# Padding rows of a routed expert layer: sixteen small stores of one engine's queue, divided between two queues

## The reference, cut to what matters

```
x = x + 0.5 * ffn(layernorm(x))
x = x + attention(layernorm(x))      # ALiBi, causal, 16 heads
x = x + 0.5 * ffn(layernorm(x))

def ffn(x):                          # E = 16 experts, each token goes to TOP_K = 4
    t = rmsnorm(x) * norm_w
    vals, idx = top_k(t @ gate_w.T + gate_b, 4)
    gates = softmax(vals)
    h = t @ w1[e] + b1[e]            # 2 * 256 columns, interleaved a and b
    act = min(a, 7) * sigmoid(1.702 * min(a, 7)) * (clip(b, -7, 7) + 1)
    return x + sum over the 4 chosen e of gates * (act @ w2[e] + b2[e])
```

## Time and profile before

| | us |
|---|---|
| median of 3 runs | 1021.15 |
| lowest, highest | 1018.97, 1021.18 |
| the profiled execution | 1019.23 |
| its span, first to last instruction | 1017.5 |
| TensorE matmuls busy | 722.9 (71%) |
| VectorE busy | 610.9 (60%) |
| ScalarE busy | 445.6 (44%) |
| GpSimd busy | 328.3 (32%) |

### The profile page before, as it was taken

The page is one execution under the profiler, slowest core; times in us unless marked ns, Lnnn a source line. Parts: engine busy times, 40 slices in busy tenths (PEclk is TensorE's granted clock), DMA queues, the critical chain, the costliest instruction groups (busy, mean ns, idle before and its releaser), DMA issues.

```text
span 1017.5 us, 22304 instructions
## 1 busy us (share of the span) xinstructions
PE 722.9 (71%) x5722; PEld 428.6 (42%) x5722; DVE 610.9 (60%) x1961; ACT 445.6 (44%) x974; POOL 328.3 (32%) x356
## 2 busy tenths in 40 slices
PE   2222079999899917778889488487129999999930
PEld 2111046666565613223343243244116666666620
DVE  6778235666555564787787368347305666665647
ACT  2534035555555524357465235261015555555510
POOL 3667713333333314101111600605512333333320
PEclk9999999999999966889999788797559999999975
DMA  9754345555444253631201313315333333333148
GB/s 311 261 212 161 136 118 167 168 168 169 131 136 127 76 176 93 197 116 49 80 18 53 132 45 130 131 44 202 118 106 99 98 99 101 95 96 91 50 133 280
DMA packets 120111, 131.63 MB, mean 129 GB/s; under 512 B 39596, under 2 KB 101525, under 8 KB 119864
## 3 DMA queue, kind: packets, MB, share of 16 engines
q1 hardware_dynamic: 101656, 91.11, 29.9%
q0 software_dynamic: 13728, 34.64, 9.5%
q10 hardware_dynamic: 4608, 4.46, 1.2%
HBM read 69.54 MB, written 64.21 MB: 131 GB/s over the span
## 4 chain that ended last, share of the span: by engine, by line
PE 44%; SPq 14%; DVE 13%; issue 13%; ACT 5%; another core or an unknown queue 5%; ACTq 3%; DMA 3%; DVEq 0%; POOLq 0%; POOL 0%
PE banks L407 13%; PE banks L429 6%; SPq L218 3%; ACT w2s L1434 3%; SPq L232 3%; SPq L217 2%; PE banks L1211 2%; PE banks L1165 2%; DVE X L727 2%; SPq L230 2%; PE banks L1277 2%; PE banks L1235 2%; PE banks L403 2%; PE banks L416 2%
## 5 line engine op out<-in xcount | busy, mean ns | idle before, releaser
L341 POOL DMA_INDIRECT y_rows<-y,goal x158 | 155.6, 985 | 318.5 <-ACT y L499 296.0
L407 PE MATMUL banks<-w1s,rT 128*128 x948 | 233.7, 383 | 0.0
L689 DVE TENSOR_SCALAR pbh<-banks 128x256 f32<-128x256 f32 x158 | 67.1, 425 | 197.3 <-ACT pbh L485 125.9
L1597 DVE CUSTOM_DVE_ANT_0 pbh<-banks,maskq 128x128 bf16<-128x128 f32 (+3 forms) x256 | 114.0, 487 | 77.8 <-PE banks L1188 46.3
L1434 ACT ACTIVATE w2s<-banks 128x1024 f32<-128x1024 f32 (+3 forms) x128 | 89.7, 701 | 123.4 <-PE banks L1219 84.3
L407 PEld LDWEIGHTS banks<-w1s,rT 128*128 128x128 f16 x948 | 93.7, 99 | 97.2 <-issue 4.0
L429 PE MATMUL banks<-w2s,hsT 128*128 x948 | 129.2, 273 | 0.0
L478 ACT ACTIVATE rT<-banks 128x512 f16<-128x512 f16 x158 | 93.5, 593 | 42.7 <-issue 34.7
L485 ACT ACTIVATE pbh<-banks 128x256 f32<-128x256 f32 x158 | 60.5, 383 | 117.3 <-PE banks L407 113.9
L1125 POOL DMA_INDIRECT x_rows<-row,row_to x64 | 61.7, 964 | 121.8 <-DVE row_to L1731 103.5
L389 PE MATMUL banks<-ident,row 128*128 128x128 f16 x632 | 62.6, 223 | 51.2 <-DMA goal<-x_rows 50.4
(11 more groups left out here) (238 smaller groups left out, 1059.7 us busy)
## 6 DMA issues: line engine op xcount, KB each, us to landing
row<-x_rows SPq DMA_DIRECT2D x158, 128.0 KB
arena<-in_w SPq DMA_DIRECT2D x16, 512.0 KB, 7.1
w1s<-y_rows SPq DMA_DIRECT2D x16, 512.0 KB, 4.7
arena<-y_rows SPq DMA_DIRECT2D x16, 512.0 KB, 7.8
qk_split<-w1s SPq DMA_DIRECT2D x48, 128.0 KB
arena<-qk_split SPq DMA_DIRECT2D x64, 96.0 KB, 2.3
w_lent<-w1s SPq DMA_DIRECT2D x22, 256.0 KB
w1s<-w_lent SPq DMA_DIRECT2D x11, 512.0 KB
```

Source lines behind the costliest of these rows:

```text
L341: pool.indirect_dma_start(y_rows[m], bass.IndirectOffsetOnAxis(ap=goal[:, n % NG, :], axis=0), y[:, n % NY, :], None, bounds_check=K * T - ...
L407: mm = pe.matmul(o, rT[:, n % 2, 2 * r + k, :], w1s[:, bass.ds(e, 1), k, w, :], start=False, stop=(k == HC - 1 and w == 1))
L689: dve.tensor_scalar(b[:, n % 2, :], bank[2 + n % 2][:, INNER:], (LIMIT + 1.0) * S, (1.0 - LIMIT) * S, ALU.min, ALU.max).then_inc(each("b"), 1)
L1597: dve.tensor_tensor_reduce(junk[:, (n * U + j) % 3, 0:W], query_bank[(n * U + j) % 3][:, 0:W], maskq[:, SEQ - W:], 1.0, -3e38, ALU.add, AL ...
```

## The change

The 16 paddings of each layer are divided. ScalarE issues those of experts 0 to 7, at the same place of its program in layer 0. In layer 1 it does so at the start of its part of the layer, that is behind the load of its gelu table and no longer ahead of it. SyncE issues those of experts 8 to 15, one behind the row loads of each of the first eight slots of a layer. The semaphores `padded` are the same in both layers, so that layer 1 waits for 64 more. The wait for all 16 in `rows_ready` is gone; instead the loads of the first 16 slots wait in groups of four in layer 1 too.

```
+PADS_FIRST = 8
+            padded = [sem(f"padded{c}") for c in range(4)]
-                padded = [ev(f"padded{c}") for c in range(4)]
+            def pad_rows(eng, e):
+                first = eng.value_load(pad_at[0:1, e:e + 1], min_val=0, max_val=(E - 1) * REGION + T)
+                eng.dma_start(x_rows[m][bass.ds(first, P), :], pad[:, :]).then_inc(padded[e // 4], 16)
...
-                    if m == 0 and n < E:
-                        sp.wait_ge(padded[n // 4], 64)
+                    if n - FIRST < E:
+                        sp.wait_ge(padded[(n - FIRST) // 4], m * 64 + 64)
...
                     load_rows(n, *(places[n] if n in places else place_of(n)))
+                    if n - FIRST < E - PADS_FIRST:
+                        pad_rows(sp, PADS_FIRST + n - FIRST)
...
                 act.preload_act_table_set("gelu_apprx_sigmoid_and_others")
-                if m == 0:
-                    act.wait_ge(route("pad_at"), 1)
-                    for e in range(E):
-                        first = act.value_load(pad_at[0:1, e:e + 1], min_val=0, max_val=(E - 1) * REGION + T)
-                        act.dma_start(x_rows[m][bass.ds(first, P), :], pad[:, :]).then_inc(padded[e // 4], 16)
+                act.wait_ge(route("pad_at"), m + 1)
+                for e in range(PADS_FIRST):
+                    pad_rows(act, e)
                 rows_out(FIRST)
...
-                sp.wait_ge(s("padded"), E * 16)
...
-                act.wait_ge(route("pad_at"), 2)
-                for e in range(E):
-                    first = act.value_load(pad_at[0:1, e:e + 1], min_val=0, max_val=(E - 1) * REGION + T)
-                    act.dma_start(x_rows[1][bass.ds(first, P), :], pad[:, :]).then_inc(s("padded"), 16)
```

## The result

The changed kernel takes 1028.57 us (median of 12 runs, 1020.05 to 1033.12) against 1021.16 (12 runs, 1016.27 to 1025.32): ratio 1.007, 95% interval 1.0042 to 1.0097. It is slower by 7.4 us. Its profiled execution took 1031.05 us with a span of 1029.3, which is 11.8 more than the span of before.

The account below looks back on a forecast made before the run. The prediction took SyncE's issue rate to bound layer 0, and in layer 1 ScalarE's paddings to delay the first row load. Layer 0 +8.6 and layer 1 -4.7 gave +3.9 us, 1025.0 against the median 1021.15, range 1016.5 to 1029.0.

Parts of the forecast that it names:

- What bounds the kernel: SyncE's issue rate sets the end of layer 0: 3.14 us a slot against TensorE's 2.72.
- Layer 0, ScalarE: Opening of layer 0: ScalarE free at 124.4, TensorE starts 4.1 us earlier, at 129.7; counts nothing in the sum.
- SyncE's start stays: Layer 0: SyncE's first row load stays at 124.07, as the paddings beside its place reads remain on ScalarE.
- The price of a padding: Each padding costs SyncE's queue 1.07 us, so eight cost it 8.6 us.
- The body of layer 0: Layer 0 to slot 69: slot time taken as unchanged, so every load behind the paddings comes 8.6 us later.
- the calm lock: Rival, 22%: SyncE and GpSimd issues don't collide in layer 0; layer 0 costs +2.5, net -2.2, 1019.0 us.
- the bad lock: Rival, 12%: slots of some 3.25 us over layer 0's lent slots; +13.4 and -4.0, about 1030.5 us.
- Layer 1: Layer 1's first load comes 8.05 us earlier, SyncE's paddings take most back; slot 8 turned 4.7 earlier, bounds 7.0 and 4.0.
- Groups of four: Waiting for paddings in groups of four on SyncE's queue costs nothing; a padding lands within 1.75 us.
- The sum: Layer 0 +8.6, layer 1 -4.7, together +3.9 us: 1025.0 against the median; own range 1022 to 1028.
- The rule of the skill: Initiating a DMA is usually small beside the DMA; by it the paddings would cost layer 0 nothing.
- the rival of free paddings: Rival, 12%: transfers, not issues, pace layer 0, which keeps its end; layer 1 gains 4.7 to 7.0, about 1015.5 us.

Follow-up runs that it names:

- e3: Kernel before, with two register reads added on SyncE behind each of the first eight row loads of layer 0, no padding moved: 975.03 us, ratio 1.0095.
- e5: Kernel before, with the two halves of each lent w1 stored by one DMA, 11 DMAs fewer on SyncE: 955.96 us against 965.09, ratio 0.9911.
- e11: Kernel before, with the 22 lent stores of layer 0 joined and issued by ScalarE instead of SyncE: 1021.65 us against 1029.40, ratio 0.9923.
- e8: Kernel before, with ScalarE's sixteen paddings of layer 0 held back until all scatters there have landed: 971.53 us, ratio 1.0063.
- e2: Kernel before, with the paddings divided in layer 0 alone, layer 1 as before: 975.35 us, ratio 1.0104.
- a2: The changed kernel run once more, same code, in the calm condition: 978.57 us against 965.09 for the kernel before, ratio 1.0143.
- e1: Kernel before, with the change in layer 1 alone, ScalarE issuing all 16 paddings in layer 0: 970.37 us against 964.85, ratio 1.0055.
- b2: Kernel before, no edit, profiled again in the slow condition: one execution, 1031.46 us.
- s1: Kernel before, with one more register read ahead of each of ScalarE's 16 paddings in layer 1: 1035.72 us against 1029.40, ratio 1.0061.
- e10: e5 with all 16 paddings on ScalarE, waited for in groups of four in both layers, layer 1's behind the gelu table load: 957.09 us, ratio 0.9915.

## Why the prediction was right, point by point

The direction came true, and for layer 0 the mechanism. The size did not: +7.4 us where +3.9 was forecast. The time lies 0.43 us inside the upper end of the range, and that it lies inside at all is partly luck.

*What bounds the kernel.* Right. That SyncE's queue sets the end of layer 0 is shown by e3 (reads alone, +8.8 us to slot 8 and +10 us in the time), e5 and e11 (instructions taken away, 9.1 and 7.8 us faster), and e8 (TensorE's start 13.5 us later, the time only 6.4).

*Layer 0, ScalarE.* Forecast 5.6 us from the first row load to the first up product, measured 5.25; worth nothing, as said.

*SyncE's start stays.* Nearly. It is 126.89, but everything began 3.9 us late; counted from the first padding it is 1.1 us earlier. That says nothing, since unsplit kernels in the same condition have 13.8 to 18.7 us between the two (16.9 in before). In the calm condition it is 20.0 to 20.1 us whether ScalarE has eight paddings (e2, a2) or sixteen (e1).

*The price of a padding* was the term most under-sized: 1.07 us forecast. In the changed kernel the distances of the row loads of slots 0 to 7 grow by 1.07 to 1.47 us, 1.23 in the mean; from the first load to slot 8 it is 23.89 us against 14.07, +9.8 and not +8.6. The smallest of the eight is the forecast value. For ScalarE's queue the row of 1.07 was a fair one: with nothing else beside, sixteen paddings took 1.03 us each (e8). What failed was to carry it over to SyncE between row loads. There the mean is 1.23, and in the calm condition 1.20 (23.85 us in e2 from the first load to slot 8, 14.27 in e1). In the dearer slots single steps are longer, as in slot 6 of e2, where the issue of the goal load takes 0.75 us and the usual one 0.33; what holds them is not shown.

*The body of layer 0.* The forecast left it as it was. The lent slots take (267.54 - 165.76) / 32 = 3.18 us against 3.14: neither the calm lock (2.95) nor the bad one (3.29). As a sign for one of them this is weak: the unsplit layer 0 of b2 and s1 had 3.27 in the same condition. Slot 69 was forecast 8.6 us later and is 10.0 later once the 3.9 of the start is taken off. TensorE's waits begin right behind the opening, 20 of them between 140 and 240 us, as foreseen.

*Layer 1.* The mechanism is right, the size was 1.0 us too good at slot 8: -4.7 forecast, -3.74 measured, just outside the bound of 4.0. (Against b2, whose paddings outlast the scatters by more, it is -5.0.) The first load is 20.87 us behind the first padding and not 20.2; from there to slot 8's load it is 23.71 us against 14.75, +8.96 and not +8.6; the latency of 2.5 us behind slot 8's load was forecast as 2.7. Another 0.4 is given back until slot 78, which leaves -3.3. What the forecast didn't say is that this gain has a condition. It is there only if ScalarE's sixteen paddings outlast the scatters: by 8.2 us in before, 9.4 in b2, 0.4 in the calm condition, where the same edit costs 5.4 us (e1).

*Groups of four.* Free (e10), and more than that. The change does two things in layer 1, and the forecast credits both together with the earlier start. The first load needs only the first four paddings, which in before are issued by 729.6, so the groups alone would have let it go as early; the division adds only SyncE's 9 us behind it. This rival, groups of four and all sixteen on ScalarE, was not run in the slow condition. An estimate from rows of before: ScalarE is free at 752.4, evicts for 0.6 us, and the first up product starts near 753.1 instead of 758.01, 4.9 us earlier, where the division gained 3.7 at slot 8 and took some 9 from SyncE's lead.

*The sum.* +3.9 forecast, +7.3 by the profiles and +7.4 by the medians. Of the 3.4 between them, layer 0 has 2.0 (10.6 for 8.6) and layer 1 has 1.4 (3.3 for 4.7), as far as two single profiles tell. 1028.57 us lies just within the range that ended at 1029.0, and 0.57 us above the 1028 at which the forecast's own range ended; by its slot time it isn't the bad lock, as far as that sign holds.

*The rule of the skill.* The Trainium skill, page "DMA: Bandwidth & Descriptors", section "Issuing engines are not separate DMA queues", calls the time of initiating DMAs usually small beside the DMA. By it the paddings would have been free on SyncE. The measurement decides against it for this kernel: eight paddings more on SyncE cost 10.5 us (e2), and sixteen register reads of the kind that goes with each padding cost 10.2 without a single DMA added (e3). With it fell the rival of free paddings.

## What to carry to other kernels

Find the queue that bounds a stage by following how its lead over the consumer shrinks, and price a DMA moved onto it by its whole string of instructions (here 1.07 us at best, 1.23 in the mean), taken as a mean over a busy stretch. Work may be moved onto the bounding queue only where a wait ends behind it that was longer than the work; measure whether that wait is there in every condition, since here it was 8 to 9 us in one and 0.4 in another, and look first whether it can go without moving any work. Where an engine's queue bounds, join its small DMAs or give them to another queue first: that made 0.9% and 0.8%, where the change lost 0.7% to 1.4%.

## What the runs showed of the hardware

The same kernel took 965.09 us (median of 13 runs) and, in the next group of runs on the same chip, 1029.40 (29 runs). In the longer condition 32 to 54 instructions of ScalarE's and SyncE's queues take about 0.70 us where there are 5 to 12 in the shorter one. Beside the last scatters of the two routings (some 20 us each, where the paddings are issued) there are 16 to 33 of them, and none in the shorter condition.

By time, something else weighs more. In all six profiles of the longer condition there are 12 to 17 waits of VectorE and ScalarE whose end the profile gives to no instruction of the core ("remote"), 54 to 85 us in total; in the eight profiles of the shorter condition there is not one. Most of this time, 42 to 74 us, lies between the layers (waits of both engines at one time count twice), as in b2, where ScalarE waits so five times (total us, times, longest):

```profile
ACT w2s L1434 <- remote: 37.0, 5, 12.9
```

Such a wait is also most of the 3.9 us by which the changed kernel reached its first padding late: VectorE stands idle for 4.29 us ahead of this step, and for 1.50 in before.

```profile
101.61 0.17 DVE L655 TENSOR_TENSOR base<-base,banks 128x16 f32<-128x16 f32 x1 [4.29 <-remote]
```

The stretch between the layers (slot 78 turned to the first padding) takes 376 to 380 us in the longer condition and 336 to 339 in the shorter, while VectorE is busy for 240 us there in both. TensorE's granted clock is lower too, 0.83 to 0.85 in that stretch against 0.87 to 0.89, but TensorE's busy time there grows by no more than 14 us (254 to 259 and 259 to 268). What makes the conditions, and what ends those waits, stays open.

A register read on SyncE with its bounds costs 0.55 us (e3), so a row load that reads two places is half reading.
